# Cross-attention, scores of 16 heads: three products over zero-padded keys, or three products over shared rows

## The chip, the cores and the metric

One core of one Trainium2 chip. The time is that of the device for one launch, in microseconds (us), the median of several runs. The trace is from one further execution that the hardware profiler recorded. Engines: TensorE (PE, with its weight loads as PEld), VectorE (DVE), ScalarE (ACT), GpSimd (POOL), SyncE (SP, which here only issues DMAs).

## The reference

Cross-attention of 32 sequences (B) of 512 rows (T) and 512 features (D) with 77 keys each (S), 16 heads of 32 features (DH), a residual (the q that is added is the input x) and a layer norm:

```
qh, kh, vh = split_heads(q @ wq.T + bq), split_heads(k @ wk.T + bk), split_heads(v @ wv.T + bv)
scores = einsum('ntd,nsd->nts', qh, kh) / sqrt(depth) + mask * PAD
out = merge_heads(softmax(scores) @ vh) + q
out = (out - mean(out)) / sqrt(var(out) + 1e-5) * gamma + beta
```

## The kernel before

Q, K and scores are computed to nearly fp32's precision out of fp32r parts: an operand is split into a high part (rounded to fp32r by ACT) and a low part (what is left, by DVE or POOL), and a product is three products, low times high, high times low and high times high, that add up in one PSUM bank.

Phase one (about 135 us) projects K and V of all sequences, eight at a time, and keeps them in DRAM scratch: `k_scratch[b, 128, 2, 4, 77]` has for each of the 128 feature rows the high and the low part of four groups g of four heads (head h of a group has rows 32h to 32h+31), `v_scratch` has V with a column of ones. It also loads x of the first sequences, keys of sequence 0, and projects the first two of the four groups of Q of sequence 0.

Phase two is a software pipeline over steps `a`. `steps` writes out the first and last ones and loops over the rest in pairs. Every engine runs its own `step(a, par)`, with eight sub-steps `s` (h = s // 4, t = s % 4); they are tied by semaphores, and each engine issues in the order of its code. PE does in a sub-step, in this order:

- `q_half` (L706): six products of 512 columns, half of a group g of Q for all 512 rows of x, into the single bank `q_ps`. Halves 0 and 1 of a group lie in two sub-steps that follow each other: part = t % 2, so the second half lies in sub-steps 1, 3, 5 and 7. Ahead of half 0 PE waits until both parts of the group before were taken out of the bank (L715, L716).
- `scores` (L726) of sequence a, heads 8h to 8h+7, rows 128t to 128t+127: for each of two groups, three products with the weights `q_hi` or `q_lo` [128 features x 128 rows] and, as the moving operand, `bd` [128 features x 4 x 77], in which head h's keys stand in rows 32h to 32h+31 of column block h and the rest is zero. The bank gets four heads x 77 scores, 308 columns.
- `turn` (L741): eight, eight, four or no transposes of the probabilities of four or eight heads in sub-steps t = 1, 2, 3 and 0; they are fp32.
- `product` (L751): probabilities times V of sequence a-1, ten fp32 instructions of 66 or 99 columns, into the single bank `o_ps`.

Around it: ACT's `high_q` (L1024) writes q_hi out of `q_ps` in the sub-step of the second half, ahead of `exponent` (L1010) of the sub-step before; it also copies turned probabilities (`copy_pt`), rounds x (`high_x`) and applies the norm. DVE's `q_low` (L868) writes q_lo out of the bank when q_hi is there, then `maximum` (L878) and `subtract_max` (L884) take the scores. POOL splits x (`split_x`), adds the residual and scales with gamma and beta (`add_rows`, `scale_rows`). SP's `step` (L669) issues in a fixed order: the keys of a+1 (`load_keys`, four DMAs: one for each head's rows, both parts and all groups at once, since `bd` has zeros elsewhere for good), x transposed of a+2, V tiles of a-1 for heads 8 to 15 (twelve DMAs), x rows of a-1, stores of a-3, V tiles of a for heads 0 to 7, stores of a-2.

## Time and profile before

| | us |
|---|---|
| median of 3 runs | 1158.64 (1158.12 to 1159.83) |
| the profiled execution's own time | 1158.84 |
| its span, first to last instruction | 1156.9 |
| PE busy in the span | 1121.3 (97%) |
| DVE, ACT, POOL busy | 820.8, 612.2, 768.8 |
| mean granted TensorE clock | 0.989 of 2.4 GHz |

The page says how long each engine was busy, which chain of work ended last, and which lines cost most. A busy share is an average over phases with different limits, so the windows view (busy time of each engine in a stretch), the waits view (who waited for whom) and the timeline (instructions in order of time) are read for one step. In a timeline "x10" merges ten instructions of one line; the second number is the length from the first's start to the last's end.

### The profile page before, as it was taken

The page shows a single profiled execution, that of the slowest core. Times are in us where ns is not written, and L with a number is a line of the kernel's source. Part 1 is how long each engine was busy: PE and PEld are TensorE (multiplying, and loading weights), DVE is VectorE, ACT ScalarE, POOL GpSimd, SP SyncE. Part 2 cuts the span into 40 slices and gives each one's busy share as a digit, 9 for nine tenths or more (in the row PEclk, how much of TensorE's full clock was granted, in tenths as well). Part 3 has the DMA queues.
Part 4 walks back from the last instruction along what each step waited for, and adds up shares of the span by engine and source line. Part 5 has one row for each costly group of instructions (what it writes and reads, how often), then busy time and mean ns, then how long its engine had stood idle before and what let it go on. Part 6 is the DMA issues. An engine that isn't in the chain of part 4 may idle for free.

```text
span 1156.9 us, 25702 instructions
## 1 busy us (share of the span) xinstructions
PE 1121.3 (97%) x7541; PEld 1036.7 (90%) x7541; DVE 820.8 (71%) x1622; ACT 612.2 (53%) x1008; POOL 768.8 (66%) x667
## 2 busy tenths in 40 slices
PE   7999799999999999999999999999999999999993
PEld 6888689999999999999999999999999999999993
DVE  6567367777777777777777777777777777777787
ACT  3221255565665555555556566555556555655551
POOL 4889623677666767666677766676766667776466
PEclk9999899999999999999999999999999999999997
DMA  7654443233344443433333333444343334334223
GB/s 228 220 188 153 161 126 89 72 100 111 119 118 125 125 125 116 124 90 108 122 124 100 111 117 116 125 125 125 116 124 99 102 119 124 106 106 117 80 88 131
DMA packets 147206, 141.05 MB, mean 122 GB/s; under 512 B 86452, under 2 KB 88004, under 8 KB 147172
## 3 DMA queue, kind: packets, MB, share of 16 engines
q1 hardware_dynamic: 146564, 140.29, 39.8%
q8 instruction: 19, 0.31, 0.1%
q10 hardware_dynamic: 608, 0.33, 0.1%
q14 instruction: 15, 0.12, 0.0%
HBM read 91.71 MB, written 48.85 MB: 122 GB/s over the span
## 4 chain that ended last, share of the span: by engine, by line
PE 84%; DVE 2%; SPq 1%; POOL 1%; issue 0%; DMA 0%; ACT 0%; DVEq 0%; POOLq 0%
PE q_ps L720 31%; PE o_ps L761 23%; PE s_ps L736 18%; PE t_ps L747 12%; SPq L647 1%; POOL x_lo L987 0%; DVE attn L849 0%; DVE y L858 0%; DVE stats L818 0%; PE q_ps L761 0%; DMA xT_raw<-in_xT 0%; DMA out<-y 0%; DVE y L864 0%; DVE y L839 0%; DVE y L842 0%
## 5 line engine op out<-in xcount | busy, mean ns | idle before, releaser
L761 PE MATMUL o_ps<-v_tiles,pt 128*128 128x66 f32 x2520 | 310.4, 270 | 1.5 <-DVE attn L810 1.5
L761 PEld LDWEIGHTS o_ps<-v_tiles,pt 128*128 128x128 f32 x2520 | 303.8, 192 | 2.0 <-issue 2.0
L881 DVE TENSOR_REDUCE row_max<-s_ps 128x8 f32<-128x616 f32 x256 | 203.5, 795 | 122.2 <-PE s_ps L736 122.1
L736 PE MATMUL s_ps<-bd,q_hi 128*128 128x308 f32 x1024 | 260.1, 305 | 1.3 <-ACT q_hi L1026 1.3
L987 POOL TENSOR_TENSOR x_lo<-xT_raw,x_hi 128x512 fp32r<-128x512 f32 x124 | 159.3, 1286 | 117.5 <-ACT x_hi L1022 117.4
L957 POOL TENSOR_TENSOR attn<-attn,x_rows 128x512 f32<-128x512 f32 x124 | 160.2, 1292 | 115.5 <-DVE attn L810 115.5
L1032 ACT COPY pt<-t_ps 128x512 f32<-128x512 f32 (+1 forms) x320 | 175.1, 588 | 105.5 <-PE t_ps L747 105.5
L720 PE MATMUL q_ps<-x_lo,wq_hi 128*128 128x512 f32 x500 | 218.7, 437 | 6.2 <-PEq L142 5.9
L1026 ACT ACTIVATE q_hi<-q_ps,bq_col 128x512 fp32r<-128x512 f32 x125 | 86.3, 690 | 254.5 <-PE q_ps L720 254.5
L1012 ACT ACTIVATE probs<-probs 128x616 f32<-128x616 f32 x256 | 183.1, 715 | 64.5 <-DVE probs L890 64.5
L890 DVE TENSOR_TENSOR probs<-s_ps,row_max 128x616 f32<-128x616 f32 x256 | 204.7, 800 | 5.7
L720 PE MATMUL q_ps<-x_hi,wq_lo 128*128 128x512 f32 x500 | 197.7, 395 | 0.0
L720 PE MATMUL q_ps<-x_hi,wq_hi 128*128 128x512 f32 x500 | 197.6, 395 | 0.0
L736 PEld LDWEIGHTS s_ps<-bd,q_hi 128*128 128x128 f32 x1024 | 181.0, 188 | 13.1 <-ACT q_hi L1026 1.7
L871 DVE SCALAR_TENSOR_TENSOR q_lo<-q_ps,bq_col,q_hi 128x512 fp32r<-128x512 f32 x125 | 93.8, 751 | 113.3 <-ACT q_hi L1026 113.3
L747 PE MATMUL t_ps<-ident,probs 128*128 128x128 f32 (+1 forms) x1280 | 171.7, 273 | 0.0
L965 POOL TENSOR_TENSOR y<-attn,gamma_all 128x512 f32<-128x512 f32 x123 | 158.5, 1289 | 12.3 <-ACT attn L1036 12.3
L968 POOL TENSOR_TENSOR y<-y,beta_all 128x512 f32<-128x512 f32 x123 | 158.7, 1290 | 9.7
L736 PE MATMUL s_ps<-bd,q_lo 128*128 128x308 f32 x512 | 156.1, 305 | 0.0
L747 PEld LDWEIGHTS t_ps<-ident,probs 128*128 128x128 f32 (+1 forms) x1280 | 150.7, 139 | 1.1
L810 DVE TENSOR_TENSOR attn<-o_ps,inv_sum 128x256 f32<-128x256 f32 x252 | 107.0, 425 | 17.9
L720 PEld LDWEIGHTS q_ps<-x_hi,wq_hi 128*128 128x128 f32 x500 | 94.1, 188 | 22.6
(96 smaller groups left out, 1287.0 us busy)
## 6 DMA issues: line engine op xcount, KB each, us to landing
xT_raw<-in_xT SPq DMA_DIRECT2D x128, 256.0 KB, 3.4
x_rows<-in_x SPq DMA_DIRECT2D x32, 1024.0 KB, 5.6
out<-y SPq DMA_DIRECT2D x128, 256.0 KB, 2.1
k_scratch<-k_out SPq DMA_DIRECT2D x8, 1232.0 KB, 5.4
bd<-k_scratch SPq DMA_DIRECT2D x128, 77.0 KB, 2.4
v_scratch<-v_out SPq DMA_DIRECT2D x16, 264.0 KB
v_tiles<-v_scratch SPq DMA_DIRECT2D x256, 9.9 KB
ctx_raw<-in_ctxT SPq DMA_DIRECT2D x3, 1232.0 KB, 9.7
```

The costliest lines, as they stand in the source:

```text
L720: mm = pe.matmul(q_bank(b, g)[:, :], (wq_hi, wq_lo)[u][:, k, P * g:P * g + P], x_part[v][:, k, :], start=(k == 0 and n == 0), stop=(k == K ...
L736: mm = pe.matmul(s_ps[t % 2][:, j, 0:GS], (q_hi, q_lo)[u][:, g, P * t:P * t + P], bd[par][:, v, g, :, :].rearrange("p h s -> p (h s)"), st ...
L747: mm = pe.transpose(t_ps[(NT * h + i) % 2][0:w, P * t:P * t + P], probs[h][:, t, P * i:P * i + w], ident[:, :])
L761: mm = pe.matmul(bank_of(b, t)[:, col:col + tile_cols[i]], pt[h][0:w, i, P * t:P * t + P], v_tiles[v_buffer(b, h)][0:w, i, 0:tile_cols[i]] ...
L881: dve.tensor_reduce(row_max[:, u, :].rearrange("p (j h) -> p j h", j=2), score_heads(t), AX.X, ALU.max).then_inc(max_ready, 1)
L890: dve.tensor_tensor(probs[h][:, t, :].rearrange("p (j h s) -> p j h s", j=2, s=S), score_heads(t), row_max[:, u, :].rearrange("p (j h) -> ...
L957: pool.tensor_tensor(attn[par][:, t, :], attn[par][:, t, :], x_rows[:, t, :], ALU.add).then_inc(resid_done, 1)
L965: pool.tensor_tensor(y[par][:, t, :], attn[par][:, t, :], gamma_all[:], ALU.mult).then_inc(scaled, 1)
L968: pool.tensor_tensor(y[par][:, t, :], y[par][:, t, :], beta_all[:], ALU.add).then_inc(out_ready, 1)
L987: pool.tensor_tensor(x_lo[par][:, k, :], xT_raw[:, k, :], x_hi[par][:, k, :], ALU.subtract).then_inc(x_lo_ready, 1)
L1012: act.activation(probs[h][:, t, :], probs[h][:, t, :], ACT.Exp).then_inc(exp_done, 1)
L1032: act.copy(pt[h][0:w, i, :], t_ps[(NT * h + i) % 2][0:w, :]).then_inc(pt_ready, 1)
```

## The change

The three products of a group of scores are built anew. A head's score is a sum of three blocks of 32 features: low Q times high K, high Q times low K, high Q times high K. For four heads these are twelve blocks, and a weight has room for four. Before, each of the three weights carried one kind of part of all four heads. Now:

- `q_a`: rows 0 to 95 hold the high parts of heads 0 to 2, rows 96 to 127 the high part of head 0 again; its moving operand `k_ac[0]` has high K of heads 0 to 2, and low K of head 0 in rows 96 to 127. 234 columns (three heads of 78).
- `q_c`: rows 0 to 95 hold the low parts of heads 0 to 2, rows 96 to 127 the high part of head 1; `k_ac[1]` has high K of heads 0 to 2, and low K of head 1. 234 columns.
- `q_b`: high part of head 3, its low part, high part of head 2, high part of head 3; `k_b` has high K of head 3 twice, low K of head 2, low K of head 3. 156 columns (two heads of 78).

A head has 78 columns instead of 77. A sub-step still has six products, with 624 instead of 924 columns for a group.

To fill them: `high_q` issues two ACTIVATEs, `q_low` two SCALAR_TENSOR_TENSORs (the second from partitions 96 to 127 to partitions 32 to 63). `move_q`, on ACT's queue, issues three DMAs within SBUF for every two groups (copies of 32 rows of Q), and `scores` waits for them (`q_moved`). `load_keys` issues twelve DMAs instead of four. `q_of_step` projects Q one sub-step further ahead: the second half of a group lies in sub-steps 0, 2, 4 and 6, and the last group of a pair is complete in sub-step 2 or 6. In ACT's `step` `exponent` now stands ahead of `high_q`.

Besides: gamma and beta are loaded at the start of phase two instead of in phase one, and DVE and POOL wait for them there; `KS` (slots of k_part) is 5 instead of 6; in phase one ACT loads the mask behind the first pieces of wk, `turn_keep` comes two groups later, and SP loads the next context ahead of storing keys and stores values between the two halves of the keys.

```diff
@@ -223,13 +241,16 @@
                 sp.dma_start(bq_col[:], bq).then_inc(consts_loaded, DMA)
-                sp.dma_start(gamma_all[:], gamma.partition_broadcast(P)).then_inc(consts_loaded, DMA)
-                sp.dma_start(beta_all[:], beta.partition_broadcast(P)).then_inc(consts_loaded, DMA)
                 for c in range(CHUNKS):
-                    store_keys(c, 0)
-                    store_keys(c, 1)
                     if c + 2 < CHUNKS:
                         load(c + 2)
+                    if c == 3:
+
+                        sp.wait_ge(x_hi_ready, KC)
+                        sp.wait_ge(x_lo_ready, KC)
+                        for k in range(KC):
+                            sp.dma_start(xT_raw[:, k, :], xT[1, P * k:P * k + P, :]).then_inc(xT_loaded[k], DMA)
+                    store_keys(c, 0)
                     if c == 0:
...
@@ -237,19 +258,15 @@
                         load_keys(0)
-                    if c == 3:
-
-                        sp.wait_ge(x_hi_ready, KC)
-                        sp.wait_ge(x_lo_ready, KC)
-                        for k in range(KC):
-                            sp.dma_start(xT_raw[:, k, :], xT[1, P * k:P * k + P, :]).then_inc(xT_loaded[k], DMA)
-                    store_values(c)
+                    store_values(c, 0, 3)
+                    store_keys(c, 1)
+                    store_values(c, 3, VT)
...
-                sp.wait_ge(consts_loaded, 3 * DMA)
+                sp.wait_ge(consts_loaded, DMA)
                 for half in range(2):
...
@@ -617,6 +651,11 @@
+            def q_of_step(s):
+
+                half, u = (s + 1) // 4, (s + 1) % 4
+                return (half + 1) // 2, (0 if half == 1 else 2) + u // 2, u % 2
+
             def in_phase_one(b, g=0):
...
@@ -660,11 +699,24 @@
                     if isinstance(b, int) and b == 1:
-                        sp.wait_ge(zeros_set, 4)
-                    for q in range(HG):
-                        rows = slice(DH * q, DH * q + DH)
-                        sp.dma_start(bd[par][rows, :, :, q, :].bitcast(F32), k_dram[b, rows, :, :, :]
+                        sp.wait_ge(zeros_set, 5)
+                    for ac in range(2):
+                        for h in range(3):
+                            rows = slice(DH * h, DH * h + DH)
+                            sp.dma_start(k_ac[par][rows, ac, :, h, 0:S].bitcast(F32), k_dram[b, rows, 0, :, :]
+                                         ).then_inc(k_loaded[par], DMA)
+                        rows = slice(DH * ac, DH * ac + DH)
+                        sp.dma_start(k_ac[par][QW:P, ac, :, ac, 0:S].bitcast(F32), k_dram[b, rows, 1, :, :]
                                      ).then_inc(k_loaded[par], DMA)
+                    for q in range(2):
+                        sp.dma_start(k_b[par][DH * q:DH * q + DH, :, 1, 0:S].bitcast(F32), k_dram[b, QW:P, 0, :, :]
+                                     ).then_inc(k_loaded[par], DMA)
+                        rows = slice(DH * (q + 2), DH * (q + 2) + DH)
+                        sp.dma_start(k_b[par][rows, :, q, 0:S].bitcast(F32), k_dram[b, rows, 1, :, :]
+                                     ).then_inc(k_loaded[par], DMA)
+
+                sp.dma_start(gamma_all[:], gamma.partition_broadcast(P)).then_inc(scale_loaded, DMA)
+                sp.dma_start(beta_all[:], beta.partition_broadcast(P)).then_inc(scale_loaded, DMA)
...
@@ -725,17 +777,21 @@
-                    pe.wait_ge(q_hi_ready, b * 4 + (2 * h + 2))
-                    pe.wait_ge(q_lo_ready, b * 4 + (2 * h + 2))
+                    pe.wait_ge(q_hi_ready, b * 8 + (4 * h + 4))
+                    pe.wait_ge(q_lo_ready, b * 8 + (4 * h + 4))
+                    pe.wait_ge(q_moved[h], (b + 1) * QDMA)
                     pe.wait_ge(k_loaded[par], b * (KDMA // 2) + (KDMA - par * (KDMA // 2)))
...
                         g = 2 * h + j
-                        for n, (u, v) in enumerate(terms):
-                            mm = pe.matmul(s_ps[t % 2][:, j, 0:GS], (q_hi, q_lo)[u][:, g, P * t:P * t + P],
-                                           bd[par][:, v, g, :, :].rearrange("p h s -> p (h s)"),
-                                           start=(n == 0), stop=(n == 2))
+                        for ac, q in ((0, q_a), (1, q_c)):
+                            pe.matmul(s_ps[t % 2][:, j, 0:3 * SW], q[:, g, P * t:P * t + P],
+                                      k_ac[par][:, ac, g, :, :].rearrange("p h s -> p (h s)"),
+                                      start=(ac == 0), stop=False, skip_group_check=True)
+                        mm = pe.matmul(s_ps[t % 2][:, j, 2 * SW:GS], q_b[:, g, P * t:P * t + P],
+                                       k_b[par][:, g, :, :].rearrange("p h s -> p (h s)"),
+                                       start=False, stop=True, skip_group_check=True)
                     mm.then_inc(scores_done, 1)
...
@@ -767,10 +823,9 @@
-                        qb = a + h
-                        g = (2 if h == 0 else 0) + t // 2
-                        if real(qb) and not in_phase_one(qb, g):
-                            q_half(qb, g, t % 2, (par + h) % 2)
+                        ahead, g, part = q_of_step(s)
+                        if real(a + ahead) and not in_phase_one(a + ahead, g):
+                            q_half(a + ahead, g, part, (par + ahead) % 2)
                         if real(a):
...
@@ -867,13 +922,16 @@
-                    dve.wait_ge(q_hi_ready, b * 4 + (g + 1))
-                    dve.scalar_tensor_tensor(out=q_lo[:, g, :], in0=q_bank(b, g)[:, :], scalar=bq_col[:, g:g + 1],
-                                             in1=q_hi[:, g, :], op0=ALU.add, op1=ALU.subtract
+                    dve.wait_ge(q_hi_ready, b * 8 + (2 * g + 2))
+                    dve.scalar_tensor_tensor(out=q_c[0:QW, g, :], in0=q_bank(b, g)[0:QW, :], scalar=bq_col[0:QW, g:g + 1],
+                                             in1=q_a[0:QW, g, :], op0=ALU.add, op1=ALU.subtract
                                              ).then_inc(q_lo_ready, 1)
+                    dve.scalar_tensor_tensor(out=q_b[DH:2 * DH, g, :], in0=q_bank(b, g)[QW:P, :],
+                                             scalar=bq_col[QW:P, g:g + 1], in1=q_b[QW:P, g, :],
+                                             op0=ALU.add, op1=ALU.subtract).then_inc(q_lo_ready, 1)
                 def score_heads(t):
-                    return s_ps[t % 2][:, :, 0:GS].rearrange("p j (h s) -> p j h s", s=S)
+                    return s_ps[t % 2][:, :, 0:GS].rearrange("p j (h s) -> p j h s", s=SW)[:, :, :, 0:S]
...
@@ -931,9 +989,9 @@
                             row_stats(*rows, 1 - par)
-                        g = (2 if h == 0 else 0) + t // 2
-                        if real(a + h) and t % 2 == 1 and not in_phase_one(a + h, g):
-                            q_low(a + h, g)
+                        ahead, g, part = q_of_step(s)
+                        if part == 1 and real(a + ahead) and not in_phase_one(a + ahead, g):
+                            q_low(a + ahead, g)
                         if rows is not None:
...
@@ -946,6 +1004,7 @@
+                dve.wait_ge(scale_loaded, 2 * DMA)
                 steps(dve, step)
...
@@ -974,11 +1033,13 @@
-                pool.memset(bd[1][:].bitcast(F32), 0.0).then_inc(zeros_set, 1)
+                pool.memset(k_ac[1][:].bitcast(F32), 0.0).then_inc(zeros_set, 1)
+                pool.memset(k_b[1][:].bitcast(F32), 0.0).then_inc(zeros_set, 1)
                 pool.memset(v_tiles[0][:], 0.0).then_inc(zeros_set, 1)
...
                 pool.memset(minus_half[:], -0.5).then_inc(half_set, 1)
+                pool.wait_ge(scale_loaded, 2 * DMA)
                 pool.wait_ge(half_set, 1)
...
@@ -1023,8 +1084,19 @@
                     act.wait_ge(q_done, b * 4 + (g + 1))
-                    act.activation(q_hi[:, g, :], q_bank(b, g)[:, :], ACT.Identity, bias=bq_col[:, g:g + 1]
+                    act.activation(q_a[0:QW, g, :], q_bank(b, g)[0:QW, :], ACT.Identity, bias=bq_col[0:QW, g:g + 1]
                                    ).then_inc(q_hi_ready, 1)
+                    act.activation(q_b[P // 2:P, g, :], q_bank(b, g)[P // 2:P, :], ACT.Identity,
+                                   bias=bq_col[P // 2:P, g:g + 1]).then_inc(q_hi_ready, 1)
+
+                def move_q(b, h):
+
+                    act.wait_ge(q_hi_ready, b * 8 + (4 * h + 4))
+                    g = slice(2 * h, 2 * h + 2)
+                    act.dma_start(q_a[QW:P, g, :].bitcast(F32), q_a[0:DH, g, :].bitcast(F32)).then_inc(q_moved[h], DMA)
+                    act.dma_start(q_c[QW:P, g, :].bitcast(F32), q_a[DH:2 * DH, g, :].bitcast(F32)
+                                  ).then_inc(q_moved[h], DMA)
+                    act.dma_start(q_b[0:DH, g, :].bitcast(F32), q_b[QW:P, g, :].bitcast(F32)).then_inc(q_moved[h], DMA)
...
@@ -1041,15 +1113,16 @@
                             high_x(a + 2, s - 3, par)
-                        g = (2 if h == 0 else 0) + t // 2
-                        if t % 2 == 1 and real(a + h) and not in_phase_one(a + h, g):
-                            high_q(a + h, g)
-
                         if s == 0:
...
                             exponent(a, (s - 1) // 4, (s - 1) % 4)
+                        ahead, g, part = q_of_step(s)
+                        if part == 1 and real(a + ahead) and not in_phase_one(a + ahead, g):
+                            high_q(a + ahead, g)
+                            if g % 2 == 1:
+                                move_q(a + ahead, g // 2)
                         if real(a - 1 + h):
...
```

## Rows read from the trace of the kernel before

**Rows 1.** The page's chain that ended last, by line: share of the span.

```profile
PE q_ps L720 31%; PE o_ps L761 23%; PE s_ps L736 18%; PE t_ps L747 12%; SPq L647 1%; POOL x_lo L987 0%; DVE attn L849 0%; DVE y L858 0%; DVE stats L818 0%; PE q_ps L761 0%; DMA xT_raw<-in_xT 0%; DMA out<-y 0%; DVE y L864 0%; DVE y L839 0%; DVE y L842 0%
```

**Rows 2.** Windows view of one step: busy us (instructions), clock, DMA share.

```profile
core 0: us, PE busy (x) PEld busy (x) DVE busy (x) ACT busy (x) POOL busy (x), PEclk, DMA share, GB/s
500.00:531.30 31.30, 31.30 (x218) 29.13 (x217) 22.70 (x47) 18.22 (x30) 21.48 (x18) 1.00 0.38 116
```

**Rows 3.** Waits, 200 to 1090 us: who for whom, us, times, longest.

```profile
DVE q_lo L871 <- ACT q_hi L1026: 103.5, 114, 1.5
```

**Rows 4.** Timeline, sub-step 1: start, length, engine, line, out<-in, idle before.

```profile
539.08 0.39 PE L720 MATMUL q_ps<-x_hi,wq_hi 128*128 128x512 f32 x1
...
539.51 0.69 ACT L1026 ACTIVATE q_hi<-q_ps,bq_col 128x512 fp32r<-128x512 f32 x1 [3.40 <-PE q_ps L720]
...
540.03 0.93 PEld L747 LDWEIGHTS t_ps<-ident,probs 128*128 128x128 f32 x8
540.09 0.71 ACT L1012 ACTIVATE probs<-probs 128x616 f32<-128x616 f32 x1
...
540.23 0.75 DVE L871 SCALAR_TENSOR_TENSOR q_lo<-q_ps,bq_col,q_hi 128x512 fp32r<-128x512 f32 x1 [0.25 <-ACT q_hi L1026]
...
540.90 0.79 DVE L881 TENSOR_REDUCE row_max<-s_ps 128x8 f32<-128x616 f32 x1
540.93 1.20 PEld L761 LDWEIGHTS o_ps<-v_tiles,pt 128*128 128x128 f32 x10
...
542.05 0.19 PEld L720 LDWEIGHTS q_ps<-x_lo,wq_hi 128*128 128x128 f32 x1
...
542.16 0.19 PEld L720 LDWEIGHTS q_ps<-x_hi,wq_lo 128*128 128x128 f32 x1
```

**Rows 5.** Timeline, a place where PE waits for q_lo.

```profile
151.65 0.75 DVE L871 SCALAR_TENSOR_TENSOR q_lo<-q_ps,bq_col,q_hi 128x512 fp32r<-128x512 f32 x1 [0.34 <-ACT q_hi L1026]
...
152.52 0.19 PEld L720 LDWEIGHTS q_ps<-x_lo,wq_hi 128*128 128x128 f32 x1 [0.20 <-issue]
```

**Rows 6.** Timeline, sub-step 0 of the same step.

```profile
535.71 0.39 PE L720 MATMUL q_ps<-x_hi,wq_hi 128*128 128x512 f32 x1
...
535.94 0.30 PE L736 MATMUL s_ps<-bd,q_hi 128*128 128x308 f32 x1
...
536.65 1.22 PEld L761 LDWEIGHTS o_ps<-v_tiles,pt 128*128 128x128 f32 x10
536.79 1.23 PE L761 MATMUL o_ps<-v_tiles,pt 128*128 128x66 f32 x10
...
537.80 0.19 PEld L720 LDWEIGHTS q_ps<-x_lo,wq_hi 128*128 128x128 f32 x1
```

**Rows 7.** Lines by form: busy us, mean ns of one, idle before.

```profile
L1032 ACT COPY pt<-t_ps 128x512 f32<-128x512 f32 x256 | 137.6, 589 | 103.4 <-PE t_ps L747 103.4
...
L1032 ACT COPY pt<-t_ps 104x512 f32<-104x512 f32 x64 | 37.5, 586 | 2.1 <-PE t_ps L747 2.0
...
L416 DVE TENSOR_TENSOR v_out<-v_ps,bv_all 128x512 f32<-128x512 f32 x16 | 10.9, 682 | 2.7 <-PE v_ps L518 2.7
...
L416 DVE TENSOR_TENSOR v_out<-v_ps,bv_all 104x512 f32<-104x512 f32 x4 | 2.7, 681 | 1.4 <-PE v_ps L518 1.4
```

**Rows 8.** Timeline of ACT's queue at the start.

```profile
0.75 1.86 ACTq L337 DMA_DIRECT2D keep<-in_mask  x4
```

**Rows 9.** DMA issues by line: count, KB each, median us to landing.

```profile
bd<-k_scratch SPq DMA_DIRECT2D x128, 77.0 KB, 2.4
...
gamma_all<-in_gamma SPq DMA_DIRECT2D x1, 256.0 KB, 5.3
```

**Rows 10.** Timeline of SP's queue in the same step.

```profile
536.37 2.99 SPq L666 DMA_DIRECT2D bd<-k_scratch  x4
539.70 1.93 SPq L677 DMA_DIRECT2D xT_raw<-in_xT  x4
541.82 5.42 SPq L647 DMA_DIRECT2D v_tiles<-v_scratch  x12
```

104 lines of the change are left out of this document (69 added, 35 removed).

## The prediction

> **What bounds the kernel now.** I read the page first. TensorE holds nearly all of the chain that ended last, in four lines: Q's projection L720, the products with V L761, the scores L736, the turns L747 [rows 1]. Next the windows view over one step of the main loop (one sequence, eight sub-steps): in 31.3 us PE is busy 31.3, with the clock at 1.00, while DVE has 22.7, ACT 18.2 and POOL 21.5 [rows 2]. So in a step time is what PE issues, and any hole in PE costs its whole length. The waits view shows no PE wait there, but it shows a hand-over: DVE's q_lo waits for ACT's q_hi, 114 times between 200 and 1090 us [rows 3]. The single bank q_ps passes PE, ACT, DVE, and back to PE. The timelines show how near that is to the path.
>
> In the sub-step of rows 4 (second of its four, two turns) the last of the six Q products starts at 539.08, q_hi at 539.51, q_lo at 540.23 and ends at 540.98; PE comes back to q_ps with the weight load at 542.05 [rows 4]. Call 539.08 the point Z. The bank is free at Z + 1.90, PE is back at Z + 2.97. What PE needs after a wait is shown where it did wait: q_lo ended at 151.65 + 0.75 = 152.40, the load started at 152.52 [rows 5]. So the hand-over takes 1.90 + 0.12 = 2.02 us, and is hidden by 0.95.
>
> **The scores.** A group (one column of heads, one t) is now three products of 308 columns; six take 536.79 - 535.94 = 0.85 us, 0.142 each [rows 6]. The new ones have 234, 234 and 156 columns. Two things can set their pace. Streaming: a product of 512 columns takes 535.94 - 535.71 = 0.23 [rows 6], 0.45 ns a column (308 give 0.46), so 0.106, 0.106, 0.071. Weight loading: ten loads ahead of short products take 542.05 - 540.93 = 1.12 us, 0.112 each, and the two fp32r loads at 542.05 and 542.16 are 0.11 apart although the bank was free [rows 4]. I take the slower of the two, 0.112 for all six: 0.67 us instead of 0.85, 0.18 less in each of 256 sub-steps, 1.42 per step. If nothing else changed, that is 32 x 1.42 = 45 us off. The bounds: streaming alone gives 0.57 per sub-step, no gain 0.85.
>
> The Trainium skill (TensorE: Matmul & The Clock Gate, Back-to-back issue gap) gives N / 2.4 + 2.5 ns for a warm product, which for these widths would be 0.53 us per sub-step and so 0.14 less than I take; felt in the four odd sub-steps alone (below), that would be 17 us less in the end. The trace disagrees where it can: 0.142 for 308 columns, where the rule says 0.131, and 0.112 for short ones.
>
> **Who makes Q's parts.** q_hi becomes two ACTIVATEs (96 and 64 partitions), q_lo two SCALAR_TENSOR_TENSORs (96 and 32 partitions), all of 512 columns. Fewer partitions are not cheaper in any row: 589 ns for 128 and 586 for 104 on ACT, 682 and 681 on DVE [rows 7]. Behind a q_hi the next ACTIVATE starts 0.58 later (540.09 - 539.51), behind a q_lo the next DVE operation 0.67 later (540.90 - 540.23) [rows 4]; without overlap it would be the whole 0.75 of an operation. I take 0.58 and 0.71. Both DVE operations wait for both ACTIVATEs, and PE's wait counts both halves. So the hand-over takes 2.02 + 0.58 + 0.71 = 3.31 us from Z.
>
> The Trainium skill (VectorE: DVE Perf Modes, Two Vector instructions with no wait between them) holds a Vector instruction until earlier ones have finished when its operands start in another group of 32 partitions than the last ones; the second q_lo reads from partition 96 and writes to 32. No operation before does this, so no row here shows it; by that rule the price is the whole 0.75, 5 us more in the end than what I take.
>
> **The move of Q.** The six products of a g are split over two sub-steps. Before, the second half lay in sub-steps 1, 3, 5, 7; with q_of_step it lies in 0, 2, 4, 6, and PE asks for q_ps again at the next sub-step's start. That is the point of this forecast: sub-steps 0 and 4 have no turns, so PE is back soonest there. Road from Z to that weight load, before: sub-step 0 takes 537.80 - 535.71 = 2.09 [rows 6]; sub-step 2 has two turns like the one of rows 4, 2.97. With shorter scores: 1.91 and 2.79. The hand-over of 3.31 is longer than both: PE waits 1.40 in sub-steps 0 and 4 and 0.52 in 2 and 6, 3.84 us per step. The score gain of 1.42 is inside this sum. Net: +2.42 us per step. For the 30 steps with every part in them: +73.
>
> The first step (scores of sequence 0, no products yet) has less to cover the hand-over: road about 0.8 in three sub-steps and 1.7 in one, so 3 x 2.5 + 1.6 = 9.1 of waits, less 1.4 and less some 0.7 it waited already: +7. The last step has one hand-over left and gains as much as it loses.
>
> **What else moves.** ACT: per step four ACTIVATEs more (2.3 us) and six DMA issues at about 0.47 [rows 8], 2.8: 18.2 to 23.3 of some 33.7. DVE: 22.7 + 2.8 = 25.5. Neither becomes the bound. exponent now stands ahead of high_q; shifted comes before it, so it runs while PE is still projecting. The moves (q_moved): the second ACTIVATE ends at Z + 1.70, three issues to 3.1, landing 2.4 to 5.3 [rows 9]: 5.5 to 8.4. The scores that need them are two sub-steps on: the hand-over 3.31, sub-step 3 about 3.6, the projection of sub-step 4 1.5, so Z + 8.4. Hidden, and this is the wait behind which scores, turns and products of PE would queue; without the projection a sub-step further ahead they would not be. Behind the issues on ACT stand the copies of two turns, done at Z + 4.1; the turn that reuses their bank comes at Z + 5.5.
>
> SP: the keys are 12 loads of 128 runs in place of 4 of 256. Before, they take 539.70 - 536.37 = 3.33, 0.83 each; xT, with 128 runs, (541.82 - 539.70) / 4 = 0.53 [rows 10]. I take 0.62: 7.4 us, 4.1 more. Behind them stand xT, the V tiles of heads 8 to 15 and x_rows. Those V tiles are all issued at 547.24 and landed by 549.6 at 2.4 [rows 10, 9]; their first product loads weights at 536.65 + 15.65 = 552.3 (half a step behind that of sub-step 0 [rows 6]), 2.7 later, and PE will be there about 1.0 later than now. So they come late by 0.4. That wait is in sub-step 4 behind Z, where PE would stand 1.40 anyway: it costs nothing up to 1.40.
>
> Phase one: its stores are reordered, k_part has one slot less, turn_keep is later; PE has no wait there that these touch, 0 within 2. DVE and POOL now wait for gamma and beta at the start of phase two (landing 5.3 after issue [rows 9]), ahead of x_lo: +2. The memsets (as many elements) and the stride of 78 in DVE's reads: nothing. That PE's clock falls is not in the sum: it stays busy nine tenths of the time.
>
> Sum: 73 + 7 + 2 = 82 on the profiled 1158.84 us (span 1156.9, 1.9 outside it; the median of the runs is 1158.64): 1240 us. A change within 0.2% (2.3 us) can't be told from none.
>
> **Rivals.**
> 1. The second halves cost little, so the hand-over stays covered, and the scores' gain is what counts. It decides at a hand-over of 2.62 (2 x (2.62 - 1.91) = 1.42), that is 0.60 added rather than 1.29. With nothing added: 2 x 0.11 of waits, -1.2 per step, about 1122 us. Against it: rows 7. 7%; another 3% lies near the point of no change.
> 2. The halves cost half of what I take (hand-over 2.9): 2 x 0.99 + 2 x 0.11 - 1.42 = 0.8 per step, about 1190. 8%.
> 3. SP becomes late: at 0.83 per key load they take 10 us, 6.7 more, V tiles are late by 3.0, of which 1.6 isn't covered: +48, 1288; x_rows would be late too, at sub-step 5. The rows leave 0.53 to 0.83 open. 17%.
> 4. Score products under some width run at fp32's price. Eight fp32 turns of 128 columns take 540.93 - 540.03 = 0.90 [rows 4], 0.88 ns a column, and an fp32 product is two instructions (ten for the five of L761): 624 columns at 1.76 are 1.10 us a group, 2.2 per sub-step for 0.85, +10.8 per step, the hand-over hidden: about 1500. No row here has fp32r under 308 columns. 3%.
>
> The forecast itself has 62%. Its own range is 1215 to 1258: the price of the second q_lo (0.67 to 0.78) is worth -5 to +8, the scores' price (only the four odd sub-steps feel it) -12 to +22, the start 3. To hold 8 in 10 the range takes in most of rival 3: 1210 to 1288. Faster: 0.07. Same: 0.03. Slower: 0.90.
>
> **What would show it.** Per step 33.7 us in place of 31.3. Score starts 0.112 apart, not 0.142. Waits of PE (or of its weight load) on q_lo: two of 1.4 and two of 0.5 per step, at 0, 2, 4, 6. Two q_hi 0.58 apart. No wait on q_moved; V tiles late by under 1.4. The forecast fails if the hand-over from Z to the next load is under 2.8, or if PE's waits are on V tiles or the moves instead.

## The result, and the profile after

The changed kernel takes 1269.93 us (median of 4 runs, 1268.52 to 1274.08), the kernel before beside it 1158.63: ratio 1.096, interval 1.094 to 1.099. The forecast was 1240, with 1210 to 1288 as its range and 1215 to 1258 as the range of its own mechanism. Direction and mechanism came as told; the loss is 111 us where 82 were forecast. The profiled execution has a span of 1269.4 us (1156.9 before), so 112.5 us are to be placed.

The page of the changed kernel: busy time by engine, the chain that ended last by engine and by line, and the costliest group.

```profile
PE 1109.2 (87%) x7541; PEld 1004.4 (79%) x7541; DVE 927.7 (73%) x1750; ACT 715.5 (56%) x1136; POOL 769.0 (61%) x669
...
PE 53%; issue 15%; DVE 11%; ACT 8%; SPq 1%; POOL 1%; DMA 0%; DVEq 0%; ACTq 0%; POOLq 0%
PE q_ps L772 30%; PE o_ps L817 11%; DVE q_b L929 7%; ACT q_b L1089 7%; PE t_ps L803 7%; PE s_ps L789 5%; PE s_ps L792 2%; ACT q_a L1087 1%; DVE q_c L926 1%; DVE row_max L939 1%; DVE probs L948 1%; DVE stats L873 0%; DVE attn L904 0%; SPq L686 0%; DMA v_tiles<-v_scratch 0%
...
L772 PE MATMUL q_ps<-x_lo,wq_hi 128*128 128x512 f32 x500 | 219.9, 440 | 116.6 <-DVE q_b L929 112.3
```

Before, four lines of PE held 84% of the chain [rows 1]; now PE has 53%, and the second halves, DVE q_b L929 and ACT q_b L1089, stand in it with 7% each. PE is busy for 12 us less. Over the whole execution it stands still for 112.3 us ahead of products into q_ps, waiting for DVE q_b L929.

The waits view from 200 to 1180 us (who for whom, us in total, times, longest):

```profile
DVE q_c L926 <- ACT q_b L1089: 172.1, 113, 2.2
...
PE q_ps L772 <- DVE q_b L929: 99.4, 112, 1.4
...
PE o_ps L817 <- DMA v_tiles<-v_scratch: 4.2, 9, 0.6
PE s_ps L789 <- DMA q_b<-q_b: 1.5, 3, 0.7
```

99.4 us of waits for the bank, 112 of them, none over 1.4; V tiles and moves of Q together 5.7. This view leaves short waits out. In the timeline of the same stretch the scores of sub-step 4 begin later than 0.23 us behind the last Q product in 10 of 28 steps, by up to 0.9 us and 4.4 us in all: there the moved parts of Q are late already, and in all but two of the steps that is hidden, because PE would stand still for the bank behind them anyway. The timeline of sub-step 0 of one step shows one such wait whole; it answers to [rows 6] and [rows 4]:

```profile
620.74 0.39 PE L772 MATMUL q_ps<-x_hi,wq_hi 128*128 128x512 f32 x1
...
620.97 0.27 PE L789 MATMUL s_ps<-k_ac,q_a 128*128 128x234 f32 x1
...
621.17 0.68 ACT L1087 ACTIVATE q_a<-q_ps,bq_col 96x512 fp32r<-96x512 f32 x1
...
621.52 0.24 PE L792 MATMUL s_ps<-k_b,q_b 128*128 128x156 f32 x1
...
621.60 1.27 PE L817 MATMUL o_ps<-v_tiles,pt 128*128 128x66 f32 x10
621.87 0.68 ACT L1089 ACTIVATE q_b<-q_ps,bq_col 64x512 fp32r<-64x512 f32 x1
...
622.59 0.75 DVE L926 SCALAR_TENSOR_TENSOR q_c<-q_ps,bq_col,q_a 96x512 fp32r<-96x512 f32 x1 [1.08 <-ACT q_b L1089]
...
623.37 0.76 DVE L929 SCALAR_TENSOR_TENSOR q_b<-q_ps,bq_col,q_b 32x512 fp32r<-32x512 f32 x1
624.15 0.80 DVE L939 TENSOR_REDUCE row_max<-s_ps 128x8 f32<-128x616 f32 x1
624.24 0.19 PEld L772 LDWEIGHTS q_ps<-x_lo,wq_hi 128*128 128x128 f32 x1 [1.52 <-issue]
```

Z is 620.74. The first q_hi starts at Z + 0.43, the second 0.70 later, the first q_lo 0.72 after that, the second 0.78 later, and 0.87 after its start PE's weight load: 3.50 us. The six score products take 621.60 - 620.97 = 0.63.

The windows view of sub-steps 0 and 1 of that step, of one whole step, and of a sub-step 1 elsewhere (busy us by engine in the order PE, PEld, DVE, ACT, POOL, with instructions; then granted clock, DMA share, GB/s):

```profile
619.48:624.27 4.79, 3.38 (x24) 3.00 (x24) 3.61 (x9) 2.09 (x3) 4.71 (x4) 1.00 0.15 55
624.27:628.30 4.03, 4.03 (x31) 3.76 (x31) 3.75 (x9) 1.79 (x3) 1.50 (x2) 1.00 0.46 79
...
653.82:688.16 34.34, 30.70 (x218) 27.79 (x218) 25.99 (x52) 21.45 (x34) 21.35 (x19) 1.00 0.51 133
...
346.37:351.97 5.60, 5.60 (x30) 5.12 (x31) 4.50 (x11) 1.99 (x4) 1.51 (x3) 0.70 0.41 79
```

A step takes 34.34 us, PE busy for 30.70; before, 31.3 and 31.30 [rows 2]. By sub-step it is 4.79, 4.02, 4.78, 3.58, twice over, where the kernel before had 3.36, 4.25, 4.25, 3.80. The last line is a sub-step 1 in which the granted clock was 0.70 in the mean: a stretch of 3.4 us at 1.2 GHz, behind a sub-step 0 with a wait of 1.4. It makes 5.60 of 4.02, and four of the thirty steps have such a stretch.

The start (from the projection of Q that ends phase one to the start of the step of sequence 1) and the end, by the same view. Changed kernel:

```profile
123.36:169.40 46.04, 32.12 (x147) 26.23 (x146) 21.16 (x28) 19.59 (x31) 15.17 (x16) 0.81 0.42 116
1206.56:1269.40 62.84, 40.55 (x288) 38.09 (x287) 47.61 (x97) 23.03 (x36) 38.15 (x31) 0.80 0.35 107
```

Kernel before, the same two stretches of its program:

```profile
123.40:158.95 35.55, 28.05 (x141) 23.41 (x140) 16.16 (x22) 15.23 (x26) 15.51 (x15) 0.90 0.44 140
1097.74:1156.90 59.16, 39.63 (x294) 37.47 (x293) 45.96 (x95) 21.37 (x34) 36.82 (x30) 0.87 0.32 107
```

The start holds six products more than before and the end six fewer (147 against 141, 288 against 294): the half of a group of Q that is now projected further ahead.

So the 112.5 us are: 30 steps between (1037.2 us against 938.8) 98.4, the start 10.5, the end 3.7. Of the 98.4, the steady step's 34.34 - 31.30 = 3.04 makes 91, the four half-clock stretches 4 x 1.6 = 6.4, and small extras the rest.

### The profile page after: what moved, and what is told of

It is laid out like the page before. It is cut to its first block, busy times and chain, and to the rows that moved or that the text cites. A ratio compares the mean times of both kernels' runs of the same rounds, so it can differ in the third digit from the quotient of the medians.

```text
span 1269.4 us, 26945 instructions
## 1 busy us (share of the span) xinstructions
PE 1109.2 (87%) x7541; PEld 1004.4 (79%) x7541; DVE 927.7 (73%) x1750; ACT 715.5 (56%) x1136; POOL 769.0 (61%) x669
## 4 chain that ended last, share of the span: by engine, by line
PE 53%; issue 15%; DVE 11%; ACT 8%; SPq 1%; POOL 1%; DMA 0%; DVEq 0%; ACTq 0%; POOLq 0%
PE q_ps L772 30%; PE o_ps L817 11%; DVE q_b L929 7%; ACT q_b L1089 7%; PE t_ps L803 7%; PE s_ps L789 5%; PE s_ps L792 2%; ACT q_a L1087 1%; DVE q_c L926 1%; DVE row_max L939 1%; DVE probs L948 1%; DVE stats L873 0%; DVE attn L904 0%; SPq L686 0%; DMA v_tiles<-v_scratch 0%
## 5 line engine op out<-in xcount | busy, mean ns | idle before, releaser
L772 PE MATMUL q_ps<-x_lo,wq_hi 128*128 128x512 f32 x500 | 219.9, 440 | 116.6 <-DVE q_b L929 112.3
L817 PE MATMUL o_ps<-v_tiles,pt 128*128 128x66 f32 x2520 | 315.6, 273 | 7.1 <-DMA v_tiles<-v_scratch 4.2
L926 DVE SCALAR_TENSOR_TENSOR q_c<-q_ps,bq_col,q_a 96x512 fp32r<-96x512 f32 x125 | 93.4, 747 | 201.8 <-ACT q_b L1089 201.8
L772 PEld LDWEIGHTS q_ps<-x_lo,wq_hi 128*128 128x128 f32 x500 | 95.2, 190 | 141.7 <-issue 127.4
L803 PE MATMUL t_ps<-ident,probs 128*128 128x128 f32 (+1 forms) x1280 | 176.2, 277 | 0.8 <-ACT pt L1104 0.8
L789 PE MATMUL s_ps<-k_ac,q_a 128*128 128x234 f32 x512 | 152.6, 298 | 6.9 <-DVE probs L948 3.8
L789 PE MATMUL s_ps<-k_ac,q_c 128*128 128x234 f32 x512 | 142.9, 279 | 0.0
L803 PEld LDWEIGHTS t_ps<-ident,probs 128*128 128x128 f32 (+1 forms) x1280 | 138.7, 141 | 0.9 <-issue 0.9
L792 PE MATMUL s_ps<-k_b,q_b 128*128 128x156 f32 x512 | 124.4, 243 | 0.0
L789 PEld LDWEIGHTS s_ps<-k_ac,q_a 128*128 128x128 f32 x512 | 99.2, 194 | 24.3 <-issue 12.9
```

The costliest lines, as they stand in the source:

```text
L772: mm = pe.matmul(q_bank(b, g)[:, :], (wq_hi, wq_lo)[u][:, k, P * g:P * g + P], x_part[v][:, k, :], start=(k == 0 and n == 0), stop=(k == K ...
L789: pe.matmul(s_ps[t % 2][:, j, 0:3 * SW], q[:, g, P * t:P * t + P], k_ac[par][:, ac, g, :, :].rearrange("p h s -> p (h s)"), start=(ac == 0 ...
L803: mm = pe.transpose(t_ps[(NT * h + i) % 2][0:w, P * t:P * t + P], probs[h][:, t, P * i:P * i + w], ident[:, :])
L817: mm = pe.matmul(bank_of(b, t)[:, col:col + tile_cols[i]], pt[h][0:w, i, P * t:P * t + P], v_tiles[v_buffer(b, h)][0:w, i, 0:tile_cols[i]] ...
```

## The experiments

### One part of the change at a time

**e3_before_split_only.** Only the split of q_hi and q_lo, in the kernel before:

```diff
-act.activation(q_hi[:, g, :], q_bank(b, g)[:, :], ACT.Identity, bias=bq_col[:, g:g + 1])
+act.activation(q_hi[0:96, g, :], q_bank(b, g)[0:96, :], ACT.Identity, bias=bq_col[0:96, g:g + 1])
+act.activation(q_hi[96:P, g, :], q_bank(b, g)[96:P, :], ACT.Identity, bias=bq_col[96:P, g:g + 1])
...
-dve.scalar_tensor_tensor(out=q_lo[:, g, :], in0=q_bank(b, g)[:, :], ...)
+dve.scalar_tensor_tensor(out=q_lo[0:96, g, :], in0=q_bank(b, g)[0:96, :], ...)
+dve.scalar_tensor_tensor(out=q_lo[96:P, g, :], in0=q_bank(b, g)[96:P, :], ...)
```

> The kernel before with one thing of the change: q_hi is made by two ACTIVATEs (96 and 32 partitions) and q_lo by two SCALAR_TENSOR_TENSORs (96 and 32 partitions), DVE and PE wait for both of each. Old keys, old scores (308 columns), old place of the projection. Same output. Theory (the halves cost what the changed trace shows): hand-over 2.02 + 0.70 + 0.78 = 3.50 against roads of 2.97 (sub-steps 1, 5) and 2.52 (3, 7): waits 2 x 0.53 + 2 x 0.98 = 3.0 per step, step 34.3, total about 1258 us (1245 to 1270). At the forecast's prices of 0.58 and 0.71: 3.31, waits 2 x 0.34 + 2 x 0.79 = 2.3, about 1230. Rival (halves of fewer partitions are cheaper, the loss is from the scores or the loads): within 1% of 1158.

Measured: 1261.60 us, ratio 1.088 (1.087 to 1.090). A step takes 34.4 us, its sub-steps 1, 3, 5 and 7 are 4.79 each. The waits view, 300 to 1000 us:

```profile
PE q_ps L720 <- DVE q_lo L874: 47.6, 82, 0.8
```

With none of the new keys, scores, loads or moves there is a loss of nine tenths the size. It is not a share of the changed kernel's loss, since PE waits in other sub-steps here, with other roads; it shows that the halves alone are enough. Their price is that of the changed trace, not the forecast's (which gave 1230).

**e4_before_move_only.** Only q_of_step, in the kernel before:

```diff
-g = (2 if h == 0 else 0) + t // 2
...
-if real(a + h) and not in_phase_one(a + h, g):
-    q_half(a + h, g, t % 2, (par + h) % 2)
+ahead, g, part = q_of_step(s)
+if real(a + ahead) and not in_phase_one(a + ahead, g):
+    q_half(a + ahead, g, part, (par + ahead) % 2)
```

> The kernel before with one thing of the change: the six products of a g lie one sub-step further ahead (second halves in sub-steps 0, 2, 4, 6 instead of 1, 3, 5, 7). Old q_hi and q_lo (one operation each), old keys and scores. Same output. The hand-over of 2.02 meets roads of 2.09 (sub-steps 0 and 4, no turns) and 2.97. Theory (the place costs nothing by itself while the hand-over is single): no wait, step 31.3, total 1156 to 1162 us. Rival (the place is a loss of its own, DVE being late behind its row statistics in sub-step 0, or ACT behind a copy): 0.2 to 0.5 per step, 1165 to 1175.

Measured: 1158.46 us, ratio 0.9994 (0.9985 to 1.0003); steps of 31.3 us, and no wait of PE between 300 and 1000 us. The new place costs nothing while the hand-over is single: 2.02 fits under 2.09.

**e5_after_old_place.** The changed kernel with Q's projection where it was:

```diff
-half, u = (s + 1) // 4, (s + 1) % 4
-return (half + 1) // 2, (0 if half == 1 else 2) + u // 2, u % 2
+h, t = s // 4, s % 4
+return h, (2 if h == 0 else 0) + t // 2, t % 2
```

> The changed kernel with the projection of Q back in its old place (second halves of the products in sub-steps 1, 3, 5, 7). Same output. The hand-over of 3.50 meets roads of 2.75 (two turns in the sub-step) and 2.30: waits 2 x 0.75 + 2 x 1.20 = 3.9 per step instead of 4.7, which alone would give 33.4 per step, about 1240 us. But the scores of the next half step now come one sub-step behind Z: at Z + 5.0, and the moved parts of Q land at about Z + 5.6 to 6.1. Theory: that adds 0.6 to 1.1 twice per step, 34.6 to 35.6 per step, total 1275 to 1310, with PE's waits named q_moved in front of the scores of sub-steps 0 and 4. Rival (the moves land sooner or the further place is a pure loss): 1235 to 1250.

Measured: 1482.32 us, ratio 1.278 (1.275 to 1.280), far over what either theory said. The waits view, 300 to 1000 us, and the landing times of the move of q_b in that stretch:

```profile
PE s_ps L789 <- DMA q_b<-q_b: 91.3, 33, 5.4
PE q_ps L772 <- DVE q_b L929: 47.5, 59, 1.2
...
DMA to landing us min/median/max: 2.4/2.5/7.2
```

The kind of wait is the one expected, its size is not: in sub-step 4 the last move, issued while V tiles and x_rows are on the queues, lands up to 7.2 us after its issue, and PE stands 5.4. Sub-step 4 takes about 10 us, and for 6.8 to 10.2 us of it and of the sub-steps behind it the clock is at 1.2 GHz (0.91 in the mean of the execution); sub-step 5 takes about 6.0 us instead of 4.8. So with SP's queue as it is the packing needs the further place of the projection; whether another order of that queue (e7, below) would do as well was not run.

### What an operation behind another costs

**e6_series_at_end.** Series of operations behind the last one of the changed kernel (its time, 1308.48 us in one run, means nothing). Shortened:

```diff
+for lo, hi in ((0, P), (0, P), (0, QW), (0, QW), (P // 2, P), (P // 2, P), (0, QW), (QW, P)):
+    act.activation(x_lo[..][lo:hi, ..], q_ps[lo:hi, :], ACT.Identity, bias=bq_col[lo:hi, 0:1])
+for lo, hi, to in (..., (0, QW, 0), (0, QW, 0), (QW, P, DH), (QW, P, DH), (QW, P, QW), (QW, P, QW), ...):
+    dve.scalar_tensor_tensor(out=tile[to:to + hi - lo, ..], in0=q_ps[lo:hi, :], ...)
+for count, cols in ((60, 512), (12, 308), (12, 234), (12, 156), (12, 78)):
+    ...  # count fp32r products of cols columns, each with other weights
```

> The changed kernel with series of operations put behind its last one; its time is the changed kernel's and some 70 us, its output the same. ACT: eight ACTIVATEs of 512 columns from the bank (128, 128, 96, 96, 64 from partition 64, the same, 96, 32 from partition 96). DVE: twelve SCALAR_TENSOR_TENSORs of 512 columns from the bank, with partitions 0-127 twice, 0-95 twice, 96-127 written to 32-63 twice, 96-127 in place twice, then 0-127, 0-95, 96-127 to 32-63, 0-127. TensorE: sixty fp32r products of 512 columns and twelve each of 308, 234, 156 and 78, every one with other weights, twice. Theory for the 0.70 and 0.78 of the changed trace, where the forecast had 0.58 and 0.71: ACT starts the next one 0.70 later whenever it reads the bank again (0.58 was an operation that reads SBUF behind one that reads the bank), whatever the partitions; DVE starts the next 0.67 later where the partitions begin in the same place and 0.78 later where they begin elsewhere, which is what the Trainium skill's rule on two Vector instructions (VectorE: DVE Perf Modes) says of another group of 32 partitions. Rival for both engines: the spacing is the same for all pairs. TensorE: by the trace 0.142 for 308 columns and 0.105 for 234, 156 and 78 alike if loading weights sets the pace; by streaming alone 0.142, 0.106, 0.071, 0.036; by N / 2.4 + 2.5 ns (the Trainium skill, TensorE: Matmul & The Clock Gate) 0.131, 0.100, 0.068, 0.035.

Measured, timeline of ACT (start, length), from the first operation on 64 partitions from 64 on, over the second, back to 96 partitions from 0 on:

```profile
1268.00 0.68 ACT L1157 ACTIVATE x_lo<-q_ps,bq_col 64x512 fp32r<-64x512 f32 x1
1268.59 0.67 ACT L1157 ACTIVATE x_lo<-q_ps,bq_col 64x512 fp32r<-64x512 f32 x1
1269.27 0.68 ACT L1157 ACTIVATE x_lo<-q_ps,bq_col 96x512 fp32r<-96x512 f32 x1
```

The second one on the same partitions starts 0.59 later, the next, at another first partition, 0.68. Over the series: 0.57 to 0.59 where the first partition stays (four pairs), 0.68 to 0.70 where it changes (three). ACT reads the bank in all of them, so the theory written down for ACT is wrong: not what it reads matters but where the partitions start. Input and output move together in every pair, so which of the two decides is open.

DVE, from 96 partitions at 0 to 32 at 96 written to 32, the same again, and 96 written in place:

```profile
1272.66 0.74 DVE L1025 SCALAR_TENSOR_TENSOR attn<-q_ps,bq_col,x_lo 96x512 f32<-96x512 f32 x1
1273.42 0.76 DVE L1025 SCALAR_TENSOR_TENSOR attn<-q_ps,bq_col,x_lo 32x512 f32<-32x512 f32 x1
1274.10 0.75 DVE L1025 SCALAR_TENSOR_TENSOR attn<-q_ps,bq_col,x_lo 32x512 f32<-32x512 f32 x1
1274.86 0.76 DVE L1025 SCALAR_TENSOR_TENSOR attn<-q_ps,bq_col,x_lo 32x512 f32<-32x512 f32 x1
```

0.76 at the change, 0.68 for the same again, 0.76 where only the output's start changes; over the series 0.66 to 0.69 (six pairs) and 0.75 to 0.77 (five). By the Trainium skill (VectorE: DVE Perf Modes, Two Vector instructions with no wait between them) an instruction is held until the earlier ones have finished when an input or the output starts in another group of 32 partitions than the last one in that memory; all eleven pairs go by that rule, and the second q_lo costs its whole 0.75 and 0.03 more.

TensorE: each row begins with the last product of the width before, so 11 products of 234 columns lie between the first two starts, and 12 of 156 between the next two:

```profile
1282.98 1.39 PE L848 MATMUL s_ps<-x_hi,q_a 128*128 128x234 f32 x11
...
1284.20 1.47 PE L848 MATMUL s_ps<-x_hi,q_a 128*128 128x234 f32 x12
...
1285.51 1.47 PE L848 MATMUL s_ps<-x_hi,q_a 128*128 128x156 f32 x12
```

0.111 for 234 columns and 0.109 for 156; inside a series of equal width 156 and 78 columns are 0.111 to 0.112 apart alike, 308 are 0.141, 512 are 0.227. So the floor of 0.112 of the forecast is there. It does not depend on the columns, and the loads ahead of short products stand as far apart [rows 4], so it is put down to the loads; nothing else was varied. A block of six is shorter than six times that: in the changed trace the sixth product starts 0.55 behind the first (620.97, 621.52), and what follows it starts 0.08 later, 0.63 in all. The Trainium skill's N / 2.4 + 2.5 ns (TensorE: Matmul & The Clock Gate, Back-to-back issue gap) gives 0.068 and 0.035 for 156 and 78 columns, and the page says itself that this leaves out the weight load; the rows disagree by far more than at 308.

### Taking the hand-over apart

**e1_other_half_first.** The same four operations in another order:

```diff
+act.activation(q_b[P // 2:P, g, :], q_bank(b, g)[P // 2:P, :], ...).then_inc(q_hi_ready, 1)
 act.activation(q_a[0:QW, g, :], q_bank(b, g)[0:QW, :], ...).then_inc(q_hi_ready, 1)
-act.activation(q_b[P // 2:P, g, :], q_bank(b, g)[P // 2:P, :], ...).then_inc(q_hi_ready, 1)
...
+dve.wait_ge(q_hi_ready, b * 8 + (2 * g + 1))
+dve.scalar_tensor_tensor(out=q_b[DH:2 * DH, g, :], in0=q_bank(b, g)[QW:P, :], ...)
 dve.wait_ge(q_hi_ready, b * 8 + (2 * g + 2))
 dve.scalar_tensor_tensor(out=q_c[0:QW, g, :], in0=q_bank(b, g)[0:QW, :], ...)
-dve.scalar_tensor_tensor(out=q_b[DH:2 * DH, g, :], in0=q_bank(b, g)[QW:P, :], ...)
```

> The changed kernel with one order turned round: ACT makes q_b (heads 2 and 3) first and q_a after it; DVE makes the low part of head 3 as soon as q_b is there, while ACT makes q_a, and the low part of heads 0 to 2 last. Same operations, same output. In the changed kernel's trace the hand-over from Z is ACT at +0.43, second ACTIVATE +0.70, first q_lo +0.72, second q_lo +0.78, ends after 0.76, weight load +0.11: 3.50 us. Theory (PE waits for this chain of four operations and for nothing else): the two middle ones now overlap, the hand-over is 0.43 + 0.70 + 0.02, then 0.78 + 0.76 + 0.11 = 2.80; sub-steps 0, 4, 2 and 6 fall from 4.79 to 4.08, a step from 34.34 to 31.5, and the total to about 1178 us (1170 to 1188). Rival (the waits belong to key loads, V tiles or moves, and only show up behind q_ps): the step stays near 34.3, total near 1270. Rival (ACT and DVE slow each other in the shared bank): each operation over 0.85 us, step near 32.5.

Measured: 1215.81 us, ratio 1.047 (1.042 to 1.051). The timeline of a sub-step 0, and of the sub-step 4 of the same step:

```profile
605.61 0.68 ACT L1090 ACTIVATE q_a<-q_ps,bq_col 96x512 fp32r<-96x512 f32 x1
605.62 0.76 DVE L926 SCALAR_TENSOR_TENSOR q_b<-q_ps,bq_col,q_b 32x512 fp32r<-32x512 f32 x1 [0.57 <-ACT q_b L1088]
...
607.27 0.19 PEld L772 LDWEIGHTS q_ps<-x_lo,wq_hi 128*128 128x128 f32 x1 [0.81 <-issue]
...
621.24 0.37 PE L789 MATMUL s_ps<-k_ac,q_a 128*128 128x234 f32 x1 [0.62 <-DMA q_b<-q_b]
...
622.93 0.77 PE L817 MATMUL o_ps<-v_tiles,pt 128*128 128x66 f32 x5 [0.80 <-DMA v_tiles<-v_scratch]
```

ACT and DVE work on the bank side by side at unchanged lengths, Z (604.47) to the load is 2.80, and sub-steps 0, 2 and 6 are 4.08 each, to the hundredth as expected. The total is not: in sub-step 4 PE now waits for the last move and then for V tiles, 4.3 to 7.1 us instead of 4.08 (300 to 1000 us), and 37.5 of these 700 us are at 1.2 GHz, where the changed kernel has 10.2. PE asks for the bank 0.7 per hand-over sooner. The moves, late by up to 0.9 in the changed kernel, are late by up to 2.0 here, and the wait for the bank no longer hides it.

**e7_half_first_queue_order.** e1 with SP's queue reordered:

```diff
-    if real(a + 1) and not in_phase_one(a + 1):
-        load_keys(a + 1, 1 - par)
     ...xT of a + 2...
     if real(a - 1) and not is_last(a - 1):
         load_v(a - 1, 1)
+    if real(a + 1) and not in_phase_one(a + 1):
+        load_keys(a + 1, 1 - par)
     ...x_rows...
```

> The kernel of e1_other_half_first with SP's queue in another order: xT, V tiles of heads 8 to 15, keys, x_rows, where it was keys, xT, V tiles, x_rows. Same loads, same output. In e1 sub-steps 0, 2 and 6 stood at 4.08 as forecast, but sub-step 4 took 4.3 to 7.1: the moved part of Q landed 5.6 us after its issue, while xT (1 MB) was under way, and V tiles after it. Theory (what is late is what stands behind the twelve key loads, and the moves share the DMA engines with xT): with xT and V tiles ahead, sub-step 4 falls to 4.08, the half-clock stretches go, step 31.5, total 1170 to 1182 us. Rival (the DMA engines are simply full, order does not matter): 1205 to 1225.

Measured: 1182.11 us, ratio 1.020 (1.018 to 1.022), at the upper edge of what was expected. From 300 to 1000 us PE waits for nothing but the bank:

```profile
PE q_ps L772 <- DVE q_c L930: 34.5, 44, 0.9
```

Steps of 31.7 us, and no half-clock stretch between 173 and 1152 us. Sub-step 4 stays at 4.30: there ACT has a high_x and an exp ahead of the hand-over, and its first part starts 0.65 behind Z instead of 0.43.

**e10_after_queue_order.** The same reorder in the changed kernel itself.

> The changed kernel with SP's queue in the order of e7 (xT, V tiles, keys, x_rows) and nothing else. Same output. Theory (key loads, V tiles and moves are hidden behind PE's waits for q_ps in the changed kernel, so the third rival of the prediction has no part in its time): the step stays at 34.3; at most the first steps and two single late V tiles gain, total 1260 to 1270 us. Rival (late loads have a share of the loss, as in e1): under 1255.

Measured: 1270.40 us, ratio 1.096 (1.094 to 1.098), steps of 34.3. The queue's order is worth nothing there, although the moves are now in time in every sub-step 4 from 200 us on: loads and moves are hidden behind PE's waits for the bank. The third rival has no part in the result.

### Freeing the bank sooner

**e2_raw_copy.** One ACTIVATE empties the bank; the parts are made from its copy:

```diff
+act.activation(q_raw[:], q_bank(b, g)[:, :], ACT.Identity, bias=bq_col[:, g:g + 1]).then_inc(q_copied, 1)
+act.copy(q_a[0:QW, g, :], q_raw[0:QW, :]).then_inc(q_hi_ready, 1)
+act.copy(q_b[P // 2:P, g, :], q_raw[P // 2:P, :]).then_inc(q_hi_ready, 1)
...
+dve.tensor_tensor(q_c[0:QW, g, :], q_raw[0:QW, :], q_a[0:QW, g, :], ALU.subtract)
+dve.tensor_tensor(q_b[DH:2 * DH, g, :], q_raw[QW:P, :], q_b[QW:P, g, :], ALU.subtract)
```

> The changed kernel with the bank emptied by one ACTIVATE: Q plus bias goes to a tile in SBUF (128 x 512, fp32), PE's next projection waits for that copy alone, and q_a, q_b (ACT) and the low parts (DVE) are made from the copy. Same output, one ACT operation more per g. Theory (the whole loss is the hand-over from Z): it becomes 0.43 + 0.69 + 0.11 = 1.2 us against roads of 1.87 and 2.75, no wait is left, and the shorter scores show at last: the step is 31.30 - 8 x 0.22 = 29.5, the total about 1110 us (1100 to 1120). Rival (ACT becomes late: 23.9 us per step with its issues, plus 2.8, out of 29.5): PE waits for copies of turns or for the moved parts, some 0.5 to 1 per step, 1125 to 1140. Rival (the price of the change is elsewhere): not under 1158.

Measured: 1391.84 us, ratio 1.201 (1.199 to 1.203). PE no longer waits for q_ps at all. From 300 to 1000 us it waits for this, and a DVE group by form (of the whole execution) shows why:

```profile
PE o_ps L818 <- DVE attn L866: 98.2, 66, 2.5
...
L929 DVE TENSOR_TENSOR q_b<-q_raw,q_b 32x512 fp32r<-32x512 f32 x126 | 142.3, 1129 | 3.9
```

DVE stands in its queue until ACT's third operation is done, then takes 1.13 us in the mean (0.68 with POOL at rest, 1.66 beside it) for what took 0.76 out of the bank; max, subtract and the attn that frees o_ps come behind. The hand-over was moved to another bank. Besides, 89 of these 700 us are at 1.2 GHz, so the 1391.84 are not the waits alone.

**e8_full_width_parts.** Another packing (heads 4, 2, 2), so that both parts are one operation of 128 partitions each, and DMAs do the rest:

```diff
+act.activation(q_a[:, g, :], q_bank(b, g)[:, :], ...)
...
+dve.scalar_tensor_tensor(out=q_l[:, g % 2, :], in0=q_bank(b, g)[:, :], ...)
...
+act.dma_start(q_b[half:P, g, :], q_a[0:half, g, :])
+act.dma_start(q_c[0:half, g, :], q_a[half:P, g, :])
+act.dma_start(q_b[0:half, g, :], q_l[0:half, :, :])
+act.dma_start(q_c[half:P, g, :], q_l[half:P, :, :])
```

> The changed kernel with another packing of the same twelve blocks: q_a holds the high parts of all four heads (one ACTIVATE of 128 partitions, 312 columns of keys), the low parts go to a tile of their own (one SCALAR_TENSOR_TENSOR of 128 partitions), and DMAs fill q_b (low and high of heads 0 and 1) and q_c (of heads 2 and 3), 156 columns of keys each; four moves of 256 KB per half step in place of three of 128 KB. SP's queue in the order of e7. Same output. Theory (the split of the hand-over is the loss): hand-over 2.02 again, against roads of 2.09 and 2.97 less 0.14, because the scores now take 2 x (0.144 + 0.105 + 0.105) = 0.71 in place of 0.85. Waits 0.07 twice; step 31.30 - 8 x 0.14 + 0.14 = 30.3; total 1125 to 1140 us. The moves of the low parts are issued at about Z + 2.5 to 3.7 and needed at Z + 8.0. Rival (they land 5.6 us later as in e1): 1.3 late in sub-step 4, with half-clock stretches, 1175 to 1195. Rival (the score price is not the columns'): no gain, 1160.

Measured: 1205.75 us, ratio 1.040 (1.038 to 1.042). The moves of q_c, 300 to 1000 us:

```profile
DMA to landing us min/median/max: 3.8/4.7/5.8
```

The hand-over fits (sub-step 0 at 3.39 where the moves are in time), but the 256 KB moves take 4.7 us to land, and most sub-steps 0 and 4 are 3.8 to 4.5, with PE waiting for the move out of q_l. The first two steps behind the start, of 39 and 38 us, add 14. Partly the rival: late moves, but no half-clock stretch between 221 and 1159 us, and a time above its 1175 to 1195.

**e9_full_width_copies and e11_copy_low_on_act.** The changed kernel's own packing; one ACTIVATE and one SCALAR_TENSOR_TENSOR of 128 partitions free the bank, and what must lie elsewhere is copied in SBUF afterwards:

```diff
+act.activation(q_a[:, g, :], q_bank(b, g)[:, :], ...).then_inc(q_hi_ready, 1)
+act.copy(q_b[P // 2:P, g, :], q_a[P // 2:P, g, :]).then_inc(q_hi_ready, 1)
...
+dve.scalar_tensor_tensor(out=q_c[:, g, :], in0=q_bank(b, g)[:, :], ...).then_inc(q_lo_ready, 1)
+dve.tensor_copy(q_b[DH:2 * DH, g, :], q_c[QW:P, g, :])     # e9
+act.copy(q_b[DH:2 * DH, g, :], q_c[QW:P, g, :])            # e11, in place of the line above
...
-at_least(pe, q_hi_ready, used * 2)
-at_least(pe, q_lo_ready, used * 2)
+at_least(pe, q_lo_ready, used * 2 - 1)
```

> The changed kernel with its own packing of the twelve blocks, but the bank emptied by one ACTIVATE of 128 partitions (all four high parts, to q_a) and one SCALAR_TENSOR_TENSOR of 128 partitions (all four low parts, to q_c). What has to lie elsewhere is copied afterwards in SBUF, off the bank: the high parts of heads 2 and 3 to q_b by ACT, the low part of head 3 to q_b by DVE; the same three moves by DMA. PE's next projection waits for the low parts in q_c alone. SP's queue in the order of e7. Same output. Theory (what costs is the chain that holds the bank): hand-over 2.02 against roads of 1.87 and 2.75, waits 0.15 twice; sub-steps 0 and 4 go from 4.08 and 4.30 in e7 to about 3.3 and 3.5, 2 and 6 from 4.08 to 4.02: 30.0 per step, total 1120 to 1138 us, faster than both kernels. Rival (ACT, with one operation of 0.62 more per g, 26 of 30 us, becomes late for the turns' copies): 1145 to 1165. Rival (the moves come too late again, as in e8, since PE reaches the scores sooner): 0.5 to 1.5 per step, 1145 to 1180.

Measured: 1188.91 us, ratio 1.027 (1.024 to 1.029), well over what was expected. The hand-over is short (sub-step 0 at 3.33); the new limit is DVE, by the waits from 300 to 1000 us and by form over the whole execution:

```profile
PE o_ps L816 <- DVE attn L864: 21.1, 65, 0.4
...
L929 DVE CAST q_b<-q_c 32x512 fp32r<-32x512 f32 x126 | 116.0, 920 | 4.3
```

> e9_full_width_copies with one thing changed: the copy of head 3's low part from q_c to q_b is made by ACT (behind its own two operations, before the last move) and not by DVE. Same output. In e9 the hand-over was short as forecast (sub-step 0 at 3.33, 4 at 3.5), but the copy on DVE took 0.42 us with POOL at rest and 1.0 to 1.3 beside POOL's operations, 0.92 in the mean, and DVE, with max and subtract behind it, gave o_ps back too late: sub-steps 1 and 5 at 4.60 in place of 4.02, 3 and 7 up to 4.5 in place of 3.57, PE's waits on DVE's attn. Theory (DVE's queue is the limit in e9): sub-steps 1 and 5 fall to 4.02 to 4.15, 7 to 3.6, step 30.0 to 30.3, total 1128 to 1145 us, faster than the kernel before. Rival (ACT takes over: 27.5 of 30 us with its issues, turns' copies 0.7 later): step 30.8 to 31.8, 1155 to 1185.

Measured: 1151.72 us, ratio 0.993 (0.992 to 0.995): 0.7% faster than the kernel before, a small gain, but all six runs lie below all runs of the kernel before. The timeline of a sub-step 0, and one step by the windows view:

```profile
602.34 0.69 ACT L1083 ACTIVATE q_a<-q_ps,bq_col 128x512 fp32r<-128x512 f32 x1 [0.23 <-PE q_ps L771]
603.06 0.75 DVE L925 SCALAR_TENSOR_TENSOR q_c<-q_ps,bq_col,q_a 128x512 fp32r<-128x512 f32 x1 [0.90 <-ACT q_a L1083]
...
603.86 0.19 PEld L771 LDWEIGHTS q_ps<-x_lo,wq_hi 128*128 128x128 f32 x1
...
600.66:631.25 30.59, 30.10 (x220) 27.80 (x218) 22.71 (x47) 23.15 (x39) 21.41 (x19) 1.00 0.53 149
```

Its last Q product starts at 601.91, so the load is at Z + 1.95, 0.05 behind the end of q_lo. A step takes 30.6 us, sub-step 4 still 3.90 (DVE's attn again, 23 waits of up to 0.5). The time is above the 1128 to 1145 expected. The start takes 40.5 us (35.6 before) and the two steps behind it 34.7 and 32.0, some 10 in all over a start as before and steps of 30.6; the rest is the step, 30.6 where 30.0 to 30.3 was expected.

## Why the prediction was right, and where its size was off

- **PE is the bound, and the hand-over of q_ps is the place.** Shown: the halves alone give 1.088 (e3), the place alone nothing (e4), and in e7 and e11 the time falls as the chain from Z shortens.
- **The range.** That the time lies in 1210 to 1288 is luck. It lies outside 1215 to 1258, the range of the mechanism that came true, and the wider range was made to take in the third rival, which had no part (e10). The narrow range is also not what its own terms give: 1240 less 5, 12 and 3 is 1220, and 1240 with 8, 22 and 3 is 1273.
- **The price of the halves.** Mis-sized, and the largest part of the miss: the terms 0.58 and 0.71 measured 0.70 and 0.78, so the hand-over is 3.50, not 3.31, and the sign "two q_hi 0.58 apart" failed. Both were read from pairs [rows 4] in which the second operation starts at the same partition as the first; those of the change do not. For DVE the prediction named the rule that says so and took the row instead; for ACT it had nothing. By the lengths of the sub-steps that is four times 0.20 per step, 24 us over 30 steps.
- **The scores.** 0.67 measured 0.63. The floor was right, but a block of six is shorter than six times the floor. Only the four odd sub-steps feel it: 0.045 less in each, 5 us.
- **The sum of a step.** 33.7 forecast, 34.34 measured; 2.42 over before became 3.04 (0.80 more, 0.18 less). Equal sub-steps 0, 2, 4, 6 of 4.79 show that in all four PE comes back before the bank is free; the last weight loads of sub-steps 0 and 2 start 1.79 and 2.66 behind Z, so that PE, 0.11 later, would be back after 1.90 and 2.77: the roads of 1.91 and 2.79 stand.
- **The clock.** "Not in the sum" failed. PE is busy for 30.70 of 34.34, nine tenths as forecast, and all the same four of thirty steps have a stretch at 1.2 GHz behind a wait: 6.4 us.
- **The start.** 9 forecast, 10.5 measured, by other means. The first product into q_ps is not later than before (133.41 us, 135.03 before), so the +2 for gamma and beta is not there. PE waits 9.6 in the first step against 1.7: 5.8 for q_ps, and 3.8 for DVE to hand back the bank of the scores, which the forecast did not have. Two more stretches are at half clock. That the sum is near 9 is luck.
- **The end.** 0 forecast, 3.7 measured, with six products fewer. PE's waits there are 7.4 against 4.7, of which one of 1.4 is the hand-over, and the clock is at 0.80 against 0.87. Why it fell more was not tried.
- **Moves of Q.** Forecast hidden with 5.5 to 8.4 against 8.4 and no wait on q_moved: the waits view has three of 1.5 us in all, and the timeline has the scores late in 10 of 28 sub-steps 4. They were hidden by the wait for the bank, not by being in time, as e1 shows. The upper bound of 5.3 for landing was too low: 6.1 in the changed kernel, 7.2 in e5.
- **SP and the third rival.** A key load took 0.51, not 0.62:

```profile
623.25 1.42 SPq L706 DMA_DIRECT2D k_ac<-k_scratch  x3
...
629.40 1.92 SPq L729 DMA_DIRECT2D xT_raw<-in_xT  x4
```

Twelve loads in 6.15 us (timeline of SP's queue). V tiles were waited for 9 times, 4.2 us; e10 settles it.
- **The other rivals.** Halves at no or half price: the spacing rows exclude both. fp32r below 308 columns at fp32's price: 0.111 for 234.

The terms add up: 82 forecast + 18.6 (the step, 30 x 0.62) + 7 (clock and small extras) + 1.5 (start) + 3.7 (end) = 113 of 112.5.

## What to carry to other kernels

Where one bank goes round three engines, count the operations between the last product into it and its release, price each with a pair that also changes its first partition, and compare with what PE has left to do until it comes back; splitting one operation into two smaller ones there costs a whole operation, and copies made after the release cost little while their engine has room (e11 against the changed kernel: 118 us; e9, with one of the copies on the busier DVE, 81). A late transfer can be hidden by the very wait that one wants to remove (moves late by up to 0.9 us in the changed kernel, at no cost; in e1 at a cost): look at it before the wait goes. A gain of fewer columns ends at a floor, 0.112 us a product here.

## What the runs showed that was not expected

- ACT also starts the next operation later where the first partition changes: 0.68 to 0.70 against 0.57 to 0.59, for 512 columns out of the bank.
- A copy of 32 partitions in SBUF on DVE took 0.42 us with POOL at rest and 1.0 to 1.35 beside POOL's two-input operations, 0.92 in the mean (e9); the two-input subtract 0.68 and 1.66 (e2). The Trainium skill (SBUF — State Buffer, SBUF: two separate sides) tells of a port pair that either engine holds for a whole instruction. The trace of e2 agrees: a subtract that starts while POOL's operation runs ends 0.55 us behind that operation's end, and POOL's takes 1.74 instead of 1.27. The same subtraction with one input in the bank took 0.75 to 0.76 whatever POOL did.
- In four of thirty steps of the changed kernel the clock was at 1.2 GHz for 3.4 us, each time behind a wait of 1.2 to 1.4 us for the bank. Every step has such waits; why these four was not tried. With waits of 5 us per step (e5) it was 6.8 to 10.2 us in nearly every step.
